# Experts on sorted 128-slot tiles, folded decay attention, and one block in the order of a time table

## The reference, cut to what matters

```python
x = x + rotary_attention(cond_attention(x, mask, cond, w0))      # 16 heads x 64, causal softmax
x = x + experts0(quaternion_rotate(x, cond, gate))               # 8 experts, top 2, 128-512-128
x = x + decay_attention(experts1(x, cond, ...))                  # 8 experts, top 2, 128-256-256-128
x = x + quantised_conv_ffn(cond_attention(x, mask, cond, w1))    # ternary weights, width-3 conv

def experts(x):                     # the reference computes all 8 and weighs 6 of them by zero
    for e in range(8):
        out += w[:, e, None] * mlp_e(x)      # w: softmax over the two largest gate logits

def decay_attention(x):             # 8 heads of 128; A is per head, lower triangular in a sequence
    q, k, v = x @ Wq.T, x @ Wk.T, x @ Wv.T
    A = (q @ k.T) / sqrt(128) * exp(G_t - G_s) * lam[level(t - s)]
    out = concat_h(A @ v) @ Wo.T + x         # then a layer norm
```

## Time and profile before

| | us |
|---|---|
| median of the runs (lowest, highest) | 715.18 (711.69, 717.57) |
| span of the profiled execution | 711.2 |
| PE busy | 558.2 |
| DVE busy | 461.7 |
| ACT busy | 295.9 |
| POOL busy | 186.7 |

### The profile page before, as it was taken

How to read it: one execution, slowest core, us unless ns; L and a number is a source line. 1 busy time by engine, 2 the same in 40 slices (tenths; PEclk the granted TensorE clock), 3 DMA queues, 4 the chain that set the end, 5 groups by cost and what they waited for, 6 DMA issues and landing times. The chain is left out here.

```text
span 711.2 us, 10053 instructions
## 1 busy us (share of the span) xinstructions
PE 558.2 (78%) x3794; PEld 397.6 (56%) x3794; DVE 461.7 (65%) x1036; ACT 295.9 (42%) x631; POOL 186.7 (26%) x147
## 2 busy tenths in 40 slices
PE   2374686569999978979879999999999678778542
PEld 2152575546665845736644767766676557656421
DVE  1369985955756487494851434667777978988663
ACT  0133354134444334444444343343555465646441
POOL 1546724610501161240301000130303043133210
PEclk9997988769999999999998999999999999999655
DMA  9200000000222211111213222112110000000000
GB/s 302 94 1 1 1 2 0 1 0 1 61 60 60 61 31 30 31 30 31 60 31 118 63 73 56 49 30 61 31 31 5 1 5 5 0 5 5 5 4 4
DMA packets 32895, 25.56 MB, mean 36 GB/s; under 512 B 6448, under 2 KB 29360, under 8 KB 32592
## 3 DMA queue, kind: packets, MB, share of 16 engines
q1 hardware_dynamic: 32368, 24.62, 11.7%
q10 hardware_dynamic: 480, 0.32, 0.2%
HBM read 24.40 MB, written 0.52 MB: 35 GB/s over the span
## 5 line engine op out<-in xcount | busy, mean ns | idle before, releaser
L450 ACT ACTIVATE hid<-PS,expert_b 128x512 f32<-128x512 f32 x128 | 87.5, 687 | 120.2 <-PE PS L418 86.9
L418 PE MATMUL PS<-featT,expert_w 128*128 128x512 f32 x192 | 98.9, 627 | 4.9 <-DVE xres L495 2.3
L434 PEld LDWEIGHTS PS<-expert_w,hid 128*128 128x128 f32 x768 | 88.7, 192 | 15.5 <-ACT hid L450 9.8
L434 PE MATMUL PS<-expert_w,hid 128*128 128x128 f32 x768 | 91.5, 276 | 0.9 <-ACT hid L450 0.9
L638 POOL TENSOR_TENSOR cond_kbd<-cond_qkv,const 128x2048 f32<-128x2048 f32 x16 | 59.9, 3741 | 63.4 <-ACT cond_qkv L723 63.3
L863 POOL TENSOR_TENSOR rot_sh<-rot_sh,const 128x1024 f32<-128x1024 f32 x16 | 52.4, 3295 | 38.4 <-DVE rot_sh L1036 38.4
L425 PE MATMUL PS<-hid,expert_w 128*128 128x512 f32 x128 | 60.8, 601 | 0.2
L418 PEld LDWEIGHTS PS<-featT,expert_w 128*128 128x128 f32 x192 | 32.0, 195 | 44.2 <-ACT hid L450 21.5
L495 DVE SCALAR_TENSOR_TENSOR xres<-PS,gatew,xres 128x128 f32<-128x128 f32 x64 | 18.0, 343 | 59.3 <-PE PS L434 59.3
L650 POOL TENSOR_SCALAR cond_st<-cond_st 128x1 f32<-128x1 f32 x16 | 5.8, 364 | 173.9 <-ACT cond_zn L738 173.7
L785 DVE STREAM_TRANSPOSE cond_ptbd<-cond_sm 32x512 f32<-32x512 f32 x64 | 45.0, 703 | 1.2
(11 more groups left out here) (221 smaller groups left out, 1092.7 us busy)
## 6 DMA issues: line engine op xcount, KB each, us to landing
expert_w<-in_moe_w_dram SPq DMA_DIRECT2D x48, 256.0 KB, 2.9
expert_w<-in_moe_w_dram SPq DMA_DIRECT2D x32, 128.0 KB, 2.5
wqk<-in_attn_qk_dram SPq DMA_DIRECT2D x2, 1024.0 KB, 6.2
wv<-in_attn_v_dram SPq DMA_DIRECT2D x2, 512.0 KB, 7.2
wout<-in_attn_out_dram SPq DMA_DIRECT2D x2, 512.0 KB, 8.4
last_b<-in_moe_last_b_dram SPq DMA_DIRECT2D x2, 512.0 KB, 6.1
xres<-in_x_dram SPq DMA_DIRECT2D x1, 512.0 KB, 5.2
cond_w<-in_cond_w_dram SPq DMA_DIRECT2D x2, 256.0 KB, 5.7
```

The lines of the kernel that those rows point to most:

```text
L418: mm = nc.tensor.matmul(full(at), w[:, P * f:P * f + P], featT[:, BANK * half:BANK * half + BANK], start=True, stop=True)
L434: mm = nc.tensor.matmul(full(at, E * j, E * j + E), h[:, 2 * layer + c, P * j:P * j + P], w[:, lo:lo + E], start=(c == 0), stop=(c == nf - 1))
L450: nc.scalar.activation(hid[e % 2][:, c, :], full(at), ACT.Relu, bias=WBIAS[g % WB][:, c:c + 1]).then_inc(ring_read[number % 2], 1)
```

## The change

**Sorted experts.** For each job, DVE picks the two experts of each token (`choose`), and PE counts with triangular matrices how many tokens before it took the same expert (`count`). From that `places` works out a row number for each of the 1024 (token, choice) pairs, in a DRAM array of 15 tiles of 128 rows, each tile of one expert: 8 tiles for the first 128 pairs of each expert and 7 (`EXTRA`) for what overflows. POOL writes the tokens to their rows (`scatter`, 8 indirect DMAs of 128 rows of 512 bytes). Then 15 slot tiles are run: SP loads the rows (`load_slots`) and the expert's weights (`load_weights`), PE transposes the tile (L687), two products (L694), two or four more (L705, L711), two or four for the result (L720), ACT copies and applies four ReLUs and copies the result, SP stores it (`store_slots`). For the 7 overflow tiles the expert's number is known only at run time: SP reads it into a register (`value_load`) and addresses the weights with it. At the end POOL fetches each token's two rows (`gather`, 8 indirect DMAs) and DVE adds them with their weights (`combine`). The last bias is one product a job (`biases`), added first. Weights are loaded 60 times in place of 32. Some slots of a tile stay unused and hold zeros or old rows.

**Folded heads.** Before the tiles, PE transposes the decay attention's weights (24 transposes of 128 columns) and makes for each head one matrix of the query and key weights and one of the value and output weights (16 products of 128 columns; `turn_weights`, `fold_weights`). Per tile there remain `project` (8 products of 128 columns), `scores` (4 of 256 columns, one per sequence), one DVE product (L1525), `times_u` (4 of 256 columns on 32 rows) and `output` (8 of 128). Also the two rotations of layer 0 and its router become one matrix `rot_w`, made in the first block; per tile one product (L1239), one copy.

**One block.** The two phases are one block. Every step of every tile or slot tile has its own number in a table `TIMES`, and each engine's list is sorted by it. Several double buffers become single (`ckbd`, `cptbd`, the shuffled rows `sh`). A function `claim` adds the waits on PSUM banks.

The diff, cut to its core:

```diff
@@ experts, PE @@
-                elif kind == "hidden":
-                    pe.wait_ge(w_loaded[g % WB], loads_up_to(g))
-                    mm = nc.tensor.matmul(full(at), w[:, P * f:P * f + P], featT[:, BANK * half:BANK * half + BANK], start=True, stop=True)
...
+            def transpose_slots(i):
+                pe.wait_ge(x_loaded[i % XB], 16 * (i // XB + 1))
+                claim(pe, (MB_[i % 2],), (m_y_ready, i + 1))
+                nc.tensor.transpose(full(MB_[i % 2], 3 * P, 4 * P), slot_x[i % XB][:], k["ident"]).then_inc(m_xT_ps, 1)
...
+            def hidden_b(i):
+                job, half, layer, s = job_of(i)
+                other = MB_[(i + 1) % 2]
+                pe.wait_ge(m_xT_ready, i + 1)
+                pe.wait_ge(w_loaded[i % WB], weights_up_to(i))
+                claim(pe, (other,), (m_b_ready, i + 1))
...
@@ banks @@
+        def claim(pe, banks, *readers):
...
+            for b in banks:
+                for reader, count in last_readers.get(b, ()):
+                    pe.wait_ge(reader, count)
+            for b in banks:
+                last_readers[b] = readers
@@ experts, SP @@
+            def load_weights(i):
...
+                if i >= WB:
+                    sp.wait_ge(m_out_ps, i - WB + 1)
...
+                    sp.wait_ge(extra_ready, job + 1)
+                    e = sp.value_load(extra[job % 2][0:1, s - EXPERTS:s - EXPERTS + 1], min_val=0, max_val=EXPERTS - 1)
+                    here = lambda name: d[f"moe{layer}_{name}"][bass.DynSlice(e, 1)]
...
+            def load_slots(i):
+                job, half, layer, s = job_of(i)
+                sp.wait_ge(scattered[job % 2], 16 * 2 * HT * (job // 2 + 1))
+                if i >= XB:
+                    sp.wait_ge(m_xT_ps, i - XB + 1)
+                sp.dma_start(slot_x[i % XB][:], xs[half][P * s:P * s + P, :]).then_inc(x_loaded[i % XB], 16)
+
+            def store_slots(i):
+                job, half, layer, s = job_of(i)
+                sp.wait_ge(m_y_ready, i + 1)
+                sp.dma_start(ys[half][P * s:P * s + P, :], slot_y[i % YB][:]).then_inc(m_stored[i % YB], 16)
@@ experts, POOL @@
+            def scatter(i):
...
+                for j in range(2):
+                    nc.gpsimd.indirect_dma_start(xs[half], bass.IndirectOffsetOnAxis(place_u[job % 2][:, j, n:n + 1], 0),
+                                                 src[:, HT * half + n, :], None).then_inc(scattered[job % 2], 16)
+
+            def gather(i):
+                job, n = divmod(i, HT)
+                half = job // 2
+                for b in range(YB):
+                    pool.wait_ge(m_stored[b], 16 * len(range(b, SLOTS * (job + 1), YB)))
...
@@ experts, DVE @@
+                nc.vector.scalar_tensor_tensor(out=to, in0=picked[:, 0, n, :], scalar=weight[job % 2][:, n, 0:1], in1=to, op0=ALU.mult, op1=ALU.add).then_inc(mix_step, 1)
+                dve.wait_ge(mix_step, own_mix.next())
+                nc.vector.scalar_tensor_tensor(out=to, in0=picked[:, 1, n, :], scalar=weight[job % 2][:, n, 1:2], in1=to, op0=ALU.mult, op1=ALU.add).then_inc(m_done, 1)
@@ rotation @@
+                nc.tensor.matmul(full(MB, 2 * P, 3 * P + EXPERTS), mxT[:], rot_w[:], start=True, stop=True).then_inc(f_ps, 1)
@@ folded heads, PE @@
+            def fold_weights(c):
...
+                for m in range(4):
+                    h = 4 * (c % 2) + m
+                    a, b = (log_nat[:, h, :], log_nat[:, LH + h, :]) if c < 2 else (log_nat[:, 2 * LH + h, :], log_wo[:, h, :])
+                    mm = nc.tensor.matmul(full(7, P * m, P * m + P), a, b, start=True, stop=True)
+                mm.then_inc(folding, 1)
...
+                for b in range(SEQ):
+                    mm = nc.tensor.matmul(full(SB_, 0, LH * S)[S * b:S * b + S, :], uT[:, P * n + S * b:P * n + S * b + S], pT[:, :, S * b:S * b + S], start=True, stop=True)
@@ order @@
-        def run_in_time_order(starts, steps, others=()):
-            todo = [(starts[n] + time, n, step) for time, step in steps for n in range(TILES)] + list(others)
+    "m_scatter": (128.8, 130.8, 132.8, 134.8, 242.1, 244.1, 246.1, 248.1, 250.1, 252.1, 254.2, 256.2, 400.7, 402.7, 404.7, 406.7),
...
+def run_in_time_order(steps):
+
+    todo = [(time, n, step) for name, step in steps for n, time in enumerate(TIMES[name])]
```

More of the change, by code:

```diff
@@ L78, in constants @@
     t, seq = p % S, p // S
+    same = seq[:, None] == seq[None, :]
     c = {}
@@ L81, in constants @@
     c["ones"] = np.ones((P, P))
-    c["upto"] = (seq[:, None] == seq[None, :]) & (t[:, None] <= t[None, :])
+    c["after"] = same & (t[:, None] > t[None, :])
+    c["before"] = p[:, None] < p[None, :]
     c["headmask"] = (p[:, None] // CD) == np.arange(CH)[None, :]
@@ L163, in build @@
         wscale = sb("wscale", [P, 2])
-        last_b = [sb(f"last_b{n}", [P, EXPERTS, E]) for n in range(2)]
         squares = sb("squares", [P, B])
@@ new lines, in weigh, with add_biases @@
+                dve.wait_ge(mix_step, own_mix.next())
+                gw = gatew[job % 2]
+                nc.vector.tensor_tensor(gw[:], chosen[job % 2][:], weight[job % 2][:].rearrange("p n j -> p j n").unsqueeze(3).to_broadcast([P, 2, HT, EXPERTS]), ALU.mult).then_inc(mix_step, 1)
+                dve.wait_ge(mix_step, own_mix.next())
+                nc.vector.tensor_tensor(gw[:, 0], gw[:, 0], gw[:, 1], ALU.add).then_inc(gate_ready, 1)
+            def add_biases(job):
+                half, layer = job // 2, job % 2
+                dve.wait_ge(biasing, 4 * job + 3)
+                rows = slice(HT * half, HT * half + HT)
+                bias = full(7).rearrange("p (n e) -> p n e", e=E)
+                if layer == 0:
+                    nc.vector.tensor_tensor(xres[:, rows, :], xres[:, rows, :], bias, ALU.add).then_inc(biasing, 1)
+                else:
+                    nc.vector.tensor_copy(acc[:, rows, :], bias).then_inc(biasing, 1)
```

1799 lines of the change are left out of this document (1003 added, 796 removed), and 40 rows, old and new, of the table TIMES.

## The result

The changed kernel took 747.73 us (median of 4 runs, 742.76 to 749.76) against 715.08 us of the kernel before beside it (4 runs, 711.69 to 717.57): ratio 1.0468, 95% interval 1.0409 to 1.0527. It is 4.7% slower; the forecast was 664. The profiled execution's span is 747.9 us. Runs more than 1.5% above the fastest of the same kernel are left out of every median, range and ratio here.

A forecast was written before the change was run, and what follows sets the result against it. PE was taken to bound the 400 us with expert work, DVE and chains between engines the rest. Stage by stage the span came to 660 against 711.2; with the runs' median 4 above the span, 664 was predicted, range 632 to 712.

The forecast's parts named there:

- The period of a slot tile: Serial chain from one slot tile's transpose to the next: 4.2 us in layer 1, 3.4 in layer 0, ends 2.9 and 5.5.
- The clock rival: Clock falls in the slot tiles; at 1.2 GHz throughout, 60 tiles cost 1.25 us more each, 75 us: 739; chance 0.10.
- jobs 1 and 2: Slot tiles running alone after tiles 4 to 7: 15 x 4.2 + 15 x 3.4 = 114 us, ending at 405.
- Job 3 on the path: Job 3 between cond, conv and attention steps: 15 slot tiles x 5.2 = 78 us, ending at 524.
- Tiles 4 to 7: Stage with job 0: 98 us of DVE plus 10 for routing and combining, at 91% occupation: 118 us, ending at 276.
- The first stage: Tiles 0 to 3: DVE work 104 us plus 4 for quantised weights; 135.5 us in place of 148.5, ending at 158.
- To job 3: From jobs 1 and 2 to job 3's first slot: gathers 8, sums and routing 13, scatters 8, landings 5, waits 7: 41 us.
- The last stage: From the second half's gates to the end, four tiles open: 118 us in place of 144, ending at 660.
- can't shrink: In the last tiles, 70 us of DVE at 74% would be 95; the first tile's chain can't shrink so: 118.
- SP's queue and the indirect DMAs: SP issues take 3.4 and 3.8 us a tile, just under the period; each POOL indirect DMA takes 1.0, 32 on the path.
- the rival of 2.2 us each: Indirect DMAs are the wait: at 2.2 us each the 32 on the path cost 38 us more, 702; chance 0.14.
- wrong if: Signs against the forecast: slot tiles above 5 us, SP waiting for nothing there, or last stage not shorter than 125 us.

The follow-up runs named there:

- Experiment six: The changed kernel with the quantising of the two conv weights on DVE moved from the first stage into jobs 1 and 2: 741.39 us, ratio 1.0366.

## Why the prediction failed

- **The period of a slot tile** was right at the full clock: 4.12 us measured for 4.2, 3.20 for 3.4. Its upper end for 1.2 GHz, 5.5, was too low: by its own terms it should have been 4.2 + 1.5 = 5.7, and 5.88 was measured in the rows above (5.83 as the median), the last 0.1 to 0.2 in the hops.
- **The clock rival** is the step that failed most. I gave it 0.10 and argued that gaps under 1 us would not lower the clock, and that at 1.2 GHz the busy share would rise again. Job 1 is the counterexample: waits of 0.81 us, PE busy 62.9 of 89 us (71%), clock 0.50 from the first slot tile to the last. The same chain with PE busy 51.8 of 63 us (82%) ran at 0.97. The share of a stretch alone doesn't tell the clock, though: job 2 began at 0.50 and came back to 1.00 with 41.8 of 57.5 us (73%), and overlapped it ran at 0.97 with 33.1 of 49 us (67%). What tips it is not settled. I had the row that spoke for it (34 of 54 us at 0.72) and explained it away. Its size: 26 us in job 1 (89.4 for 63), 1.7 us a tile where I had priced 1.25, and 6 in job 2, whose first four tiles ran at 3.8 to 6.2 us. That is all but 1 of the 33 us by which jobs 1 and 2 missed, and a little over a third of the whole miss. The rival's own 739 lies near the measured 748 by luck: it put 75 us on all 60 slot tiles, while 32 fell on the 30 of jobs 1 and 2 and the rest of the miss came from the steps below.
- **Job 3 on the path** (0) is a step that came true in the number only: leaving out 14 of its 15 slot tiles gave 2 us, at a clock that fell with them.
- **Tiles 4 to 7** (+12): my 118 us counted on DVE at 91%; it was busy 85.5 of 129.7 us (66%), and in the chain that ended last it has 34 us there, PE 41.
- **The first stage** (+16) took 127 us of DVE, not 108. Quantising took 8.5 us, not 4: two of its instructions took 4.9 us, one of them 3.8 beside POOL. The rest is work on tiles 4 and 5 that the table puts there, whose return in the next stage I had counted in full. Experiment six shows that only 2.4 us of the quantising were on the path, though DVE has 102.5 of the 155 us in the chain that ended last. What holds this stage and the next is not settled: the natural test is a second buffer for the spread keys and the turned probabilities of cond, as before, and it wasn't tried.
- **To job 3** (+16): eight indirect DMAs take 10.2 us, not 8, twice. The other 12 us are open: the rows point at the order of PE's list and at DVE beside POOL, and the one change of order that was run brought the rows 6 us earlier but left the handoff at 61 us.
- **The last stage** (+9): my "can't shrink" was a chain of one tile. The chain is of three tiles through one set of conv buffers, 15.8 us each, and it can shrink by 16.
- **SP's queue and the indirect DMAs**: the rival of 2.2 us each fell. The register load was cheaper than assumed. The Trainium skill, page "DMA: Bandwidth & Descriptors", section "Latency and other measured facts", puts such a load at 600 ns at least; these 28 loads took 262 to 474 ns, so the measurement decides. Its fixed 2.0 us per DMA issued from GpSimd (section "Anatomy of one DMA — SWDGE (gpsimd) path") isn't contradicted, since it counts completion, but a batch of eight overlaps it: 1.27 us apiece.
- **Of "wrong if"**: slot tiles above 5 us (they were, 5.88), the last stage not under 125 (it was 127.3), SP without a wait (it did wait).

## What to carry to other kernels

When a change empties PE, read what clock the half-empty stretches of the trace have had, and price each stage that will stand alone at both levels: the serial chain here took 5.83 us a slot tile at the one and 4.12 at the other. Work that is cheaper but serial is dear where it stands alone: before summing it, ask which of its stages have cover. And when a stage is cut away to learn its price, read the clock beside the time, since the one can hide the other. The better remedy here was to overlap two links of the chain by two more banks and a new order (40 us); added work gave 31 where it stood in waits and nothing where it stood in the chain. A step moved ahead in one engine's list gained nothing while the next engine's list held its successor.
